# A segmented scan over edges: TensorE adds four edges for the last five chunks, and three steps change place

## The reference, cut to what matters

```python
out1 = segment_sum(edge_attr, col)          # per destination node
out2 = segment_max(edge_attr, col)          # 0 where a node has no edge
out3 = out1 / max(count, 1)
h = concat([xn, out1, out2, out3, u])       # xn = layernorm(x)
gnn = relu(h @ W1 + b1) @ W2 + b2 + xn      # "the node network"
mix = attention-like product of q, k, v of xn   # (v + q2 @ kv) @ W_out + b_out
x = x + gnn + mix
x = x + ffn(layernorm(x))                   # on the 3124 nodes of highest router weight
```

## Time and profile before

| | |
|---|---|
| runs | 1189.02, 1189.10, 1190.23 us; median 1189.1 |
| profiled execution | 1189.02 us, its span 1187.3 us |
| granted TensorE clock, mean | 0.92 of full speed |
| PE busy | 1017.3 us, 86% of the span |
| DVE busy | 1009.9 us, 85% |
| ACT busy | 500.1 us, 42% |
| POOL busy | 463.0 us, 39% |
| q1 | 157.00 MB, q10 44.71 MB, q0 33.61 MB |

### The profile page before, as it was taken

The page is one execution under the profiler, slowest core; times in us unless marked ns, Lnnn a source line. Parts: engine busy times, 40 slices in busy tenths (PEclk is TensorE's granted clock), DMA queues, the critical chain, the costliest instruction groups (busy, mean ns, idle before and its releaser), DMA issues.

```text
span 1187.3 us, 15899 instructions
## 1 busy us (share of the span) xinstructions
PE 1017.3 (86%) x4571; PEld 762.9 (64%) x4571; DVE 1009.9 (85%) x2424; ACT 500.1 (42%) x1487; POOL 463.0 (39%) x344
## 2 busy tenths in 40 slices
PE   3287699999988669178999999999999985799996
PEld 1154456655645445057888888888888982488886
DVE  6899999999999999977988889888897768576574
ACT  3557587777842244431322333223332323243341
POOL 0078840888400000476664446644443000223331
PEclk9599899999995879679999999999999996599998
DMA  9899999999988999732443324443233130111110
GB/s 320 310 316 365 348 352 370 353 360 366 349 309 321 391 408 387 257 97 67 156 129 126 128 83 155 133 129 129 83 131 114 56 113 17 37 36 42 45 43 20
DMA packets 95983, 236.02 MB, mean 199 GB/s; under 512 B 13121, under 2 KB 68710, under 8 KB 89650
## 3 DMA queue, kind: packets, MB, share of 16 engines
q1 hardware_dynamic: 50450, 157.00, 35.7%
q10 hardware_dynamic: 31248, 44.71, 10.7%
q0 software_dynamic: 14224, 33.61, 10.0%
HBM read 154.72 MB, written 80.55 MB: 198 GB/s over the span
## 4 chain that ended last, share of the span: by engine, by line
PE 49%; DVE 3%; POOL 2%; issue 1%; DMA 0%; ACT 0%; DVEq 0%; POOLq 0%
PE psR L67 5%; PE psC L67 5%; PE psQ L56 5%; PE psQ L57 5%; PE psKx L56 5%; PE psQ L58 5%; PE psKx L57 5%; PE psKx L58 4%; PE psR L68 3%; PE psC L68 2%; PE psT L2120 1%; PE psQ L2141 1%; PE psKx L2141 1%; POOL graw L468 1%; PE psR L66 1%
## 5 line engine op out<-in xcount | busy, mean ns | idle before, releaser
L468 POOL DMA_INDIRECT graw<-in_edge_attr,ic x98 | 141.1, 1440 | 75.9 <-DVE ob L993 40.7
L990 DVE SCALAR_TENSOR_TENSOR ob<-ob,mQ,mx 128x96 f32<-128x96 f32 x392 | 122.4, 312 | 4.4
L993 DVE SCALAR_TENSOR_TENSOR ob<-ob,kQ,xb 128x96 f32<-128x96 f32 x392 | 122.2, 312 | 0.1
L671 POOL DMA_INDIRECT near<-ends_d,blki x49 | 87.7, 1790 | 72.1 <-DVEq L898 57.5
L671 POOL DMA_INDIRECT near<-in_dst,rowi x49 | 87.8, 1792 | 59.7 <-DVEq L907 45.1
L1789 ACT ACTIVATE hT_hi<-psQ 128x512 fp32r<-128x512 f32 (+2 forms) x52 | 29.8, 573 | 183.0 <-PE psQ L2141 155.7
L1929 PE MATMUL psQ<-Wqk,xT 128*128 128x512 f32 (+1 forms) x196 | 97.2, 620 | 0.0
L978 DVE TENSOR_TENSOR xb<-xb 128x1536 f32<-128x1536 f32 x49 | 86.1, 1758 | 1.7
L976 DVE TENSOR_TENSOR mx<-xb 128x1536 f32<-128x1536 f32 x49 | 85.6, 1747 | 1.2 <-DVE carry L1048 0.2
L67 PE MATMUL psR<-W2w,hT_hi 128*128 128x512 f32 x175 | 65.5, 410 | 3.8 <-DVE x L1156 3.8
L1789 ACT ACTIVATE hT_hi<-psKx 128x512 fp32r<-128x512 f32 (+2 forms) x52 | 29.8, 573 | 90.9 <-PE psKx L2141 84.7
(11 more groups left out here) (521 smaller groups left out, 3238.8 us busy)
## 6 DMA issues: line engine op xcount, KB each, us to landing
xb<-in_edge_attr SPq DMA_DIRECT2D x49, 1536.0 KB, 10.7
scan_d<-ob SPq DMA_DIRECT2D x49, 768.0 KB
yrow_d<-yr SPq DMA_DIRECT2D x48, 132.0 KB
xg<-in_x ACTq DMA_DIRECT2D x12, 512.0 KB
xT_d<-xT ACTq DMA_DIRECT2D x12, 512.0 KB
base_d<-dcur ACTq DMA_DIRECT2D x12, 512.0 KB
qT_d<-qT ACTq DMA_DIRECT2D x12, 512.0 KB
out_x<-xres SPq DMA_DIRECT2D x48, 128.0 KB
```

The source lines that it names most:

```text
L468: nc.gpsimd.indirect_dma_start(out=to.rearrange("p i f -> p (i f)"), out_offset=None, in_=raw_v, in_offset=bass.IndirectOffsetOnAxis(ap=ic ...
L671: nc.gpsimd.indirect_dma_start(out=near[:, t, :], out_offset=None, in_=table, in_offset=bass.IndirectOffsetOnAxis(ap=rows[:, t:t + 1], axi ...
L990: nc.vector.scalar_tensor_tensor(o[:, q, 0:EF], prev[:, 0:EF], mQ[:, bass.ds(c * TQ + q, 1)], mx[:, q, 0, :], ALU.min, ALU.max).then_inc(s ...
L993: nc.vector.scalar_tensor_tensor(o[:, q, EF:AGG], prev[:, EF:AGG], kQ[:, bass.ds(c * TQ + q, 1)], X[:, q, 0, :], ALU.mult, ALU.add).then_i ...
```

## The change

Four things change.

1. For chunks 44 to 48 VectorE leaves out the two sums of the tree. TensorE makes the sum of a quad's four edges as four accumulating products with the identity matrix, for four quads at once (384 columns), into the banks `psR` (quads 0 to 3) and `psC` (quads 4 to 7); VectorE's running sum reads it there. The new products stand in TensorE's queue behind the attention, the tail parts and the spreading of the ends. That one moves from `psR` to `psT[0]`, and waits for the attention's last rows to be read.
2. SP's weight loads come three chunks earlier (36 to 39), with their two waits. `ends_of_segments` moves from chunk 38 to 36, `rows_to_gather` from 41 to 39, `masks` from 43 to 41.
3. The gathers of group 0's raw rows signal one semaphore per tile of 128 nodes (two gathers each), the ones that the last network uses later, so its wait there becomes 48. `masked_rows` waits for a tile at a time.
4. The five loads that ScalarE issues ahead of `masked_rows` (`xTr[1]`, `bg` and `tg` of groups 0 and 1) are issued behind it.

```diff
+SUMS = (44, 45, 46, 47, 48)
+            psS = [psR, psC]
-            def gather_raw(e, nt, rows, done):
+            def gather_raw(e, nt, rows, done, each=False):
...
-                            in_offset=...ic[e][0:rows, i, t:t + 1], axis=0)).then_inc(done, 16)
+                            in_offset=...ic[e][0:rows, i, t:t + 1], axis=0)).then_inc(done[t] if each else done, 16)
...
                 if g == 0:
-                    engine.wait_ge(s_g0[t], 16)
+                    engine.wait_ge(s_g0[t], 32 + 16)
...
                     dump_and_load(c, c % XB, c + XB < CHUNKS)
-                    if c == 39:
+                    if c == 36:
                         sp.wait_ge(s_at, 6 + KF)
                         sp.wait_ge(s_fs, TILES)
-                    if c in (39, 40):
-                        for i in range(2 * (c - 39), 2 * (c - 39) + 2):
+                    if c in (36, 37):
+                        for i in range(2 * (c - 36), 2 * (c - 36) + 2):
                             sp.dma_start(rW1[:, i, :], W1[i * P:(i + 1) * P, :]).then_inc(s_wl[i], 16)
-                    elif c == 41:
+                    elif c == 38:
                         sp.dma_start(rW2[:, :, 1, :], ...).then_inc(s_wl[4], 16)
-                    elif c == 42:
+                    elif c == 39:
...
-                early(0, s_g0r)
+                early(0, s_g0, True)
...
@@ edge_chunk
+                    on_pe = c in SUMS
+                    n0 = sum(2 if k in SUMS else 4 for k in range(c))
...
-                    dve.wait_ge(s_tree, c * 4 + 1)
-                    nc.vector.tensor_tensor(xp[:, :, :, 0, :], xp[:, :, :, 0, :], xp[:, :, :, 1, :], ALU.add).then_inc(s_tree, 1)
+                    dve.wait_ge(s_tree, n0 + 1)
+                    if not on_pe:
+                        nc.vector.tensor_tensor(xp[:, :, :, 0, :], xp[:, :, :, 0, :], xp[:, :, :, 1, :], ALU.add).then_inc(s_tree, 1)
                     nc.vector.tensor_tensor(mx[:, :, 0, :], mx[:, :, 0, :], mx[:, :, 1, :], ALU.max).then_inc(s_tree, 1)
-                    dve.wait_ge(s_tree, c * 4 + 2)
-                    nc.vector.tensor_tensor(X[:, :, 0, :], X[:, :, 0, :], X[:, :, 2, :], ALU.add).then_inc(s_tree, 1)
+                    if not on_pe:
+                        dve.wait_ge(s_tree, n0 + 2)
+                        nc.vector.tensor_tensor(X[:, :, 0, :], X[:, :, 0, :], X[:, :, 2, :], ALU.add).then_inc(s_tree, 1)
...
                     for q in range(TQ):
+                        if on_pe and q % 4 == 0:
+                            dve.wait_ge(s_pt, 4 + SUMS.index(c) * 2 + q // 4 + 1)
+                        quad_sum = psS[q // 4][:, q % 4 * EF:(q % 4 + 1) * EF] if on_pe else X[:, q, 0, :]
...
                         nc.vector.scalar_tensor_tensor(o[:, q, EF:AGG], prev[:, EF:AGG], kQ[:, bass.ds(c * TQ + q, 1)],
-                                                       X[:, q, 0, :], ALU.mult, ALU.add).then_inc(s_sum, 1)
+                                                       quad_sum, ALU.mult, ALU.add).then_inc(s_sum, 1)
...
-                    if c == 38:
+                    if c == 36:
                         ends_of_segments()
+                    if c == 39:
+                        rows_to_gather()
                     if c == 41:
-                        rows_to_gather()
-                    if c == 43:
                         masks()
...
-                        step(nc.vector.tensor_scalar(leads[:, :], psR[:, :], fixf[:, 0:1], None, ALU.is_equal))
+                        step(nc.vector.tensor_scalar(leads[:, :], psT[0][:, :], fixf[:, 0:1], None, ALU.is_equal))
...
@@ masked_rows
-                    act.wait_ge(s_g0r, 32 * GT)
...
                     for t in range(GT):
+                        act.wait_ge(s_g0[t], 32)
...
+                def quad_sums(c):
+                    pe.wait_ge(s_load[c % XB], c // XB * 16 + 16)
+                    for h in range(2):
+                        if c != SUMS[0]:
+                            pe.wait_ge(s_sum, (c - 1) * TQ + 4 * h + 5)
+                        for i in range(4):
+                            ins = nc.tensor.matmul(psS[h][:, 0:4 * EF], ident[:, :], xb[c % XB][:, 4 * h:4 * h + 4, i, :],
+                                                   start=(i == 0), stop=(i == 3))
+                        ins.then_inc(s_pt, 1)
...
                 for i in range(4):
                     tail_part(i)
+                pe.wait_ge(s_t2, TILES)
                 pe.wait_ge(s_lead, 1)
-                nc.tensor.matmul(psR[:, :], ones[:, :], endrow[:, :], start=True, stop=True).then_inc(s_t, 1)
+                nc.tensor.matmul(psT[0][:, :], ones[:, :], endrow[:, :], start=True, stop=True).then_inc(s_t, 1)
+                for c in SUMS:
+                    quad_sums(c)
```

More of the change, by code:

```diff
@@ L377, in build @@
             s_ic = sem("b_ic")
-            s_g0r = sem("b_g0r")
             s_g0s = sem("b_g0s")
@@ L469, in gather_raw @@
                             out=to.rearrange("p i f -> p (i f)"), out_offset=None, in_=raw_v,
-                            in_offset=bass.IndirectOffsetOnAxis(ap=ic[e][0:rows, i, t:t + 1], axis=0)).then_inc(done, 16)
+                            in_offset=bass.IndirectOffsetOnAxis(ap=ic[e][0:rows, i, t:t + 1], axis=0)).then_inc(done[t] if each else done, 16)
             def gather_chosen(g, t, done):
@@ L686, in _, with early @@
                 pool.wait_ge(s_ic, 2)
-                def early(e, done):
+                def early(e, done, each):
                     pool.wait_ge(s_max, (46 + e) * TQ + 1)
                     pool.wait_ge(s_sum, (46 + e) * TQ + 1)
-                    gather_raw(e, GT, P, done)
-                early(0, s_g0r)
+                    gather_raw(e, GT, P, done, each)
+                early(0, s_g0, True)
                 pool.wait_ge(s_neutral_out, 48)
@@ L700, in _ @@
                 pool.wait_ge(s_as, 2)
-                early(1, s_ga[1])
+                early(1, s_ga[1], False)
                 pool.wait_ge(s_fixo, 2)
@@ L973, in edge_chunk @@
                     xp = X[:, :, :, :].rearrange("p q (h two) f -> p q h two f", two=2)
+                    on_pe = c in SUMS
+                    n0 = sum(2 if k in SUMS else 4 for k in range(c))
                     dve.wait_ge(s_load[b], g * 16 + 16)
                     nc.vector.tensor_tensor(mx[:, :, :, :], xp[:, :, :, 0, :], xp[:, :, :, 1, :], ALU.max).then_inc(s_tree, 1)
-                    dve.wait_ge(s_tree, c * 4 + 1)
-                    nc.vector.tensor_tensor(xp[:, :, :, 0, :], xp[:, :, :, 0, :], xp[:, :, :, 1, :], ALU.add).then_inc(s_tree, 1)
+                    dve.wait_ge(s_tree, n0 + 1)
+                    if not on_pe:
+                        nc.vector.tensor_tensor(xp[:, :, :, 0, :], xp[:, :, :, 0, :], xp[:, :, :, 1, :], ALU.add).then_inc(s_tree, 1)
                     nc.vector.tensor_tensor(mx[:, :, 0, :], mx[:, :, 0, :], mx[:, :, 1, :], ALU.max).then_inc(s_tree, 1)
-                    dve.wait_ge(s_tree, c * 4 + 2)
-                    nc.vector.tensor_tensor(X[:, :, 0, :], X[:, :, 0, :], X[:, :, 2, :], ALU.add).then_inc(s_tree, 1)
-                    if not isinstance(c, int) or c >= OB:
+                    if not on_pe:
+                        dve.wait_ge(s_tree, n0 + 2)
+                        nc.vector.tensor_tensor(X[:, :, 0, :], X[:, :, 0, :], X[:, :, 2, :], ALU.add).then_inc(s_tree, 1)
+                    if c >= OB:
                         dve.wait_ge(s_dump[b % OB], g * 32 + (b // OB) * 16)
-                    dve.wait_ge(s_tree, c * 4 + 4)
+                    dve.wait_ge(s_tree, n0 + (2 if on_pe else 4))
                     for q in range(TQ):
                         prev = oprev[:, TQ - 1, :] if q == 0 else o[:, q - 1, :]
+                        if on_pe and q % 4 == 0:
+                            dve.wait_ge(s_pt, 4 + SUMS.index(c) * 2 + q // 4 + 1)
+                        quad_sum = psS[q // 4][:, q % 4 * EF:(q % 4 + 1) * EF] if on_pe else X[:, q, 0, :]
                         dve.wait_ge(s_max, c * TQ + q + 1)
@@ L1759, in _ @@
                 masked_rows()
+                for e in range(2):
+                    if e == 1:
+                        act.dma_start(xTr[e][:, :, :], xT_d[e:e + 1, :, :, :].rearrange("o p c n -> p (o c) n")).then_inc(s_ld[e], 16)
+                    for to, src in ((bg[e], base_d), (tg[e], att_d)):
+                        act.dma_start(to[:, :, :], src[e * GT * P:(e + 1) * GT * P, :].rearrange("(t p) f -> p t f", p=P)).then_inc(s_lb[e], 16)
                 def node_stage():
@@ L2099, in _ @@
                 ins.then_inc(s_t, 1)
-                pe.wait_ge(s_t2, TILES)
                 pe.wait_ge(s_lead, 2)
```

## The result

The changed kernel takes 1194.24 us (median of 18 runs, 1190.18 to 1202.32) and the kernel before, on the same chip, 1188.41 (18 runs, 1186.32 to 1191.43). The ratio is 1.0042, 95% interval 1.0031 to 1.0054: about 5 us slower. The forecast was 1193.3, 4.3 us slower. The profiled execution took 1195.73 us (span 1194.0).

What follows compares the result with a forecast made beforehand. VectorE's scan was taken to bound the kernel until about 503 us, then TensorE from 557. VectorE's 16.4 us stop outweighs 12.75 saved; POOL's release comes 4.3 later: 1189.0 + 4.3 = 1193.3 us, range 1177 to 1199.

Steps and rivals of the forecast that it cites:

- Sums on TensorE: Chunks 44 to 48: VectorE saves 2.55 us each, taking 6.5 us a chunk; TensorE spends 5.1 us a chunk.
- Rival D: TensorE's clock falls to 1.2 GHz, its sums take 10.2 us a chunk and bound the kernel: 1211 us, chance 0.03.
- When TensorE gets there, and the moves: Before chunk 44's sums: moves bring 5 us, first sum ready at 475.8, VectorE stands 16.4 us.
- The formula: The shift is the moment of the first sum less 471.5; some −12.3 us for any first sum up to 459.4.
- the byte count: Queues from 384 to 456.5: q1 carries 20.3 MB, q10 8.1 of its 9.0 MB, placing the last operand at 462.
- The last attention group at 462 behind a DMA: On TensorE, the last attention group starts at 462 after waiting for its operand to land; 467.23 before.
- No stop of ScalarE for `rW`: Weights sent out behind chunks 36 to 39 take away ScalarE's 13.21 us stop for them before 424.21.
- A: The attention is really freed: q10 keeps its rate, first sum at 459.1, VectorE never waits; 1176.7 us, chance 0.17.
- B: q1 runs late by a pair of chunk transfers, first sum at 465.8, shift −5.7; 1183.3 us, chance 0.22.
- C: The last operand's landing stays at 467, first sum at 480.8; 1198.3 us, chance 0.14.
- Raw rows by tile: After the scan's chunk 45: eight gathers take 12.8 us, masks end at 514.8 against 509.9, the piece itself 6 us shorter.
- Loads moved behind the masking: ScalarE's five DMA issues, 3.2 us, delay TensorE's next stage by 8.1 us, hidden by its stop and POOL's shift.

Runs made afterwards that it cites:

- e1: The changed kernel with the sums of only chunks 46 to 48 on TensorE; 1184.85 us, ratio 0.9956 to the kernel before.
- e8: The changed kernel with only chunks 46 to 48 summed on TensorE and the five loads back ahead of the masks; 1181.75 us, ratio 0.9955.
- e10: The changed kernel with two fetches (for attention groups 8 and 11) issued from GpSimd's queue instead of ScalarE's; 1193.51 us, ratio 1.0031.
- e4: The changed kernel with the weight loads back at chunks 39 to 42; 1201.33 us, ratio 1.0104.
- e7: The changed kernel with only the five loads put back ahead of the masks; 1194.30 us, ratio 1.0047.
- e2: The changed kernel with no sums on TensorE, only the moves and the signal by tile; 1196.02 us, ratio 1.0039.
- e6: The changed kernel with the five chunks' sums put earlier in TensorE's order and the five loads back ahead of the masks; 1189.27 us, ratio 1.0010.
- e9: e8 with the sums of chunks 40 and 42 also on TensorE, ahead of attention groups 5 and 8; 1188.83 us, ratio 0.9989.
- e11: e8 with the sums of chunk 45 on TensorE as well, so chunks 45 to 48; 1186.92 us, ratio 0.9968.
- e12: e8 with the weight loads back at chunks 39 to 42; 1188.48 us, ratio 0.9986.
- e5: The changed kernel with no sums on TensorE and the five loads back ahead of the masks; 1190.62 us, ratio 1.0020.
- e3: The changed kernel with the same five sums put earlier in TensorE's order, among attention groups and tail parts; 1194.93 us, ratio 1.0037.

## Why the prediction was right

**Sums on TensorE.** Right in size: 2.55 us and 6.5 us a chunk (`L979` in chunks 45 and 46 at 480.77 and 487.24), 5.16 us of TensorE's time (forecast: 5.1), 0.51 us for the late second half (forecast: 0.7), all at a granted clock of 1.00 from 480 to 507. Rival D did not come. The clock does fall to 0.50 in e1 and e8, after 3.0 and 3.9 us without work for TensorE, and there it cost VectorE nothing.

**When TensorE gets there, and the moves.** The formula held, the shift being (first sum − 471.5): 476.5 gives 5.0, and the scan ended 4.9 us later. The first sum was forecast to within 0.7 us, and the operand's landing at 462 too: it was 461.2. But by the split of the bytes, 19.66 and 8.98 MB against a forecast of 20.3 and 8.1, q10 would have been through at 456.5, so the byte count does not place the landing as closely as it looks. And two errors cancelled behind it. The last group began at 464.5, not at 462, and it did not wait for its operand but for TensorE's own queue, which had been full since 443.1; and from there on it took 12.0 us and not 13.8, since TensorE had no idle time before it and the four tail parts took 7.3 us (465.39 to 472.73) at the full clock; before, the first two products alone took 1.92 us instead of 1.02. "The last attention group at 462 behind a DMA" is wrong, both in the time and in the wait. "No stop of ScalarE for `rW`" is right, yet two stops in the issue stand in its place, which the working did not have; e10 shows that two of them less on ScalarE bring nothing. The moves' 5 us are shown (e4: 4.9 on the first sum). That the first sum came out within 0.7 us is in part luck.

**Rivals A, B, C.** A would have had the first sum at 459.1, B at 465.8 and C at 480.8; it was at 475.7 to 476.5 in three runs that have it (e7, e10 and the changed kernel), and at C's place with the weights late.

**Raw rows by tile.** The gathers took 11.5 us (forecast 12.8), and the masks ended at 513.04 (forecast 514.8). The Trainium skill's GPSIMD Engine Reference (1. Specifications) names GpSimd's contention with VectorE instructions of two SBUF inputs. The trace agrees with that: with the chain's sums from PSUM the gathers after the first start 1.25 us apart but for one, and in e2, where they are in SBUF again, all eight take 15.05 us, to the hundredth what they took before. But the two sums of the tree, which also read two operands in SBUF, went and came back in the same kernels, so no run says which of the two made the gathers shorter.

**Loads moved behind the masking.** Here the step failed in kind, and only by luck did that hardly show in the sum. It priced ScalarE's issue time, 3.2 us; that was nothing, as the issues lie beside masks that still run (`tailT` came at 513.06, right behind them). It did not ask what the 2.6 MB collide with on the rings. In the changed kernel they go out 1.2 us behind the last dump and cost 1.3 us in the traces. Had the sums come in time, they would have gone out ahead of it and cost 3 to 4.

**Sum.** Forecast +4.3. The traces give 4.9 at the scan's end and 1.8 after it, of which 1.3 is the loads (e7); the ratio gives 5.0. The run with no sums at all (e2) is as slow as the changed kernel. That doesn't make the stop harmless: without the loads' part, no sums, three and five chunks stand at 1.0020, 0.9955 and 1.0047.

## What to carry to other kernels

Work handed to another engine is worth what it saves less the stop until that engine gets to its first piece. If the engine is not free by then, hand over fewer pieces: here three chunks gave 0.45% and five lost 0.4%, while sums put earlier in TensorE's queue (e6) or into its gaps (e9) gained nothing over the three. Where the DMA rings are full, a transfer moved up delays others (here it removed a stop of 13.2 us and brought the first sum forward by only 5), and an engine that is freed asks for its data sooner: count bytes per queue up to the moment that matters, and then ask whether the engine that needs them is free at that moment. A transfer that looks off the path is priced by what it stands ahead of, and that changes when something else gets faster.

## What the runs showed of the hardware that was not expected

- With both queues loaded, a DMA issue of ScalarE's took up to 9.33 us instead of 0.4 to 0.7, and the instructions behind it stood. With two such issues put on another engine, others of its issues took 5.14, 3.21, 3.32 and 5.53 us.
- The last dump was used 4.0 us after the scan's last instruction where the large loads had been issued 10 us or more ahead (e6 to e9, e11, e12; in e5 it was 5.8, unexplained), 4.5 where 2.6 MB were issued 0.6 to 1.2 us behind it (the changed kernel, e1), and 9.1 to 9.7 where they were issued up to 3 us ahead of it (e2, e3).
- GpSimd's eight gathers took 15.05 us beside VectorE's tree sums and chain sums in SBUF, and 11.5 where the tree sums were gone and the chain sums read one operand from PSUM. Which of the two did it is open.
- TensorE had nothing to do for 3.0 us up to 479.9 (e1) and for 3.9 us up to 479.7 (e8). Its granted clock was 1.00 before that, 0.50 from 481 to 483, and 1.00 again from 484 on.
